# Unread matrix products on TensorE ahead of and inside the expert steps of a conv-attention-MoE kernel

## What is computed

```
probs = softmax(x @ gate_w + gate_b)            # 16 experts
top_probs, top_idx = top_k(probs, 2), made to sum to 1
hidden = silu(x @ w1[e]) * (x @ w2[e])          # 64 -> 128
out    = sum over the two experts e of a token: top_probs * (hidden @ w3[e])
```

## Time and profile before

| what | value |
|---|---|
| median of 3 runs | 426.78 us (426.09 to 432.75) |
| the profiled execution | 428.84 us |
| its span, first to last instruction | 427.0 us |
| mean granted clock of TensorE | 0.835 of full |
| PE / DVE / ACT / POOL busy | 83% / 64% / 43% / 38% of the span |

### The profile page before, as it was taken

The page is one execution under the profiler, slowest core; times in us unless marked ns, Lnnn a source line. Parts: engine busy times, 40 slices in busy tenths (PEclk is TensorE's granted clock), DMA queues, the critical chain, the costliest instruction groups (busy, mean ns, idle before and its releaser), DMA issues. The chain is left out here.

```text
span 427.0 us, 8539 instructions
## 1 busy us (share of the span) xinstructions
PE 355.6 (83%) x2739; PEld 192.9 (45%) x2739; DVE 272.6 (64%) x567; ACT 183.0 (43%) x409; POOL 161.9 (38%) x171
## 2 busy tenths in 40 slices
PE   1588999989999999999999974987851199999970
PEld 0452353343353443534433223676850177777750
DVE  2489977848978879877778996378642033333323
ACT  2684654644646656635656001454311033333330
POOL 3173332332333243233331003015777246666660
PEclk9999999978999999999999997899555555555555
DMA  8859998998885958828859400000002156555415
GB/s 263 337 116 216 322 216 220 343 221 219 202 218 98 218 130 185 232 50 212 204 119 215 114 2 0 0 2 13 27 26 71 38 121 138 123 123 118 107 35 147
DMA packets 55219, 61.50 MB, mean 144 GB/s; under 512 B 23028, under 2 KB 35372, under 8 KB 55056
## 3 DMA queue, kind: packets, MB, share of 16 engines
q1 hardware_dynamic: 43712, 53.52, 49.8%
q10 hardware_dynamic: 8944, 5.41, 4.9%
q0 software_dynamic: 2528, 2.14, 1.6%
HBM read 11.95 MB, written 11.83 MB: 56 GB/s over the span
## 5 line engine op out<-in xcount | busy, mean ns | idle before, releaser
L684 DVE TENSOR_TENSOR prod<-ps_t,a_rep 128x1024 f32<-128x1024 f32 x128 | 151.9, 1218 | 35.9 <-PE ps_t L384 29.8
L791 POOL TENSOR_TENSOR a<-a,mask 128x512 f32<-128x512 f32 (+1 forms) x40 | 46.7, 1169 | 87.8 <-ACT a L544 85.6
L384 PE MATMUL ps_t<-b,vt 32*128 32x512 f32 x512 | 74.0, 647 | 2.1 <-DVE prod L684 2.1
L404 PE MATMUL ps_d<-prod,keep 128*32 128x512 f32 x512 | 69.2, 613 | 3.0 <-DVE prod L684 2.8
L325 PEld LDWEIGHTS ps_m<-om_r,sel 128*128 128x128 f32 x193 | 29.2, 189 | 76.1 <-ACT mask L522 28.2
L1257 POOL DMA_INDIRECT parts<-y_sb,x_in x47 | 45.9, 978 | 35.8 <-issue 25.9
L325 PE MATMUL ps_m<-om_r,sel 128*128 128x256 f32 x193 | 49.6, 336 | 0.0
L768 POOL TENSOR_TENSOR om_r<-om_f,om_r 56x512 fp32r<-56x512 f32 x16 | 20.4, 1273 | 55.4 <-ACT om_r L511 55.3
L1522 PE MATMUL ps_s<-xs,w_in 64*128 64x128 f32 x94 | 37.3, 499 | 0.0
L1523 PE MATMUL ps_p<-xs,w_in 64*128 64x128 f32 x94 | 37.3, 499 | 0.0
L1149 DVE TENSOR_TENSOR hidden<-ps_p,gated 128x128 f32<-128x128 f32 x47 | 13.7, 291 | 36.1 <-ACT gated L1351 36.1
(11 more groups left out here) (151 smaller groups left out, 489.4 us busy)
## 6 DMA issues: line engine op xcount, KB each, us to landing
a_rep<-a SPq DMA_DIRECT2D x128, 256.0 KB, 4.9
rows<-blank SPq DMA_DIRECT2D x8, 1056.0 KB, 6.9
w_in<-in_experts ACTq DMA_DIRECT2D x47, 96.0 KB, 2.1
a_rep<-a SPq DMA_DIRECT2D x32, 128.0 KB, 2.7
x_in<-rows SPq DMA_DIRECT2D x47, 33.0 KB, 1.9
x_in<-rows SPq DMA_DIRECT2D x47, 32.0 KB, 1.8
start<-in_start SPq DMA_DIRECT2D x1, 1344.0 KB, 7.8
parts<-y_sb,x_in POOLq DMA_INDIRECT x47, 2.8
```

The lines of the kernel that those rows point to most:

```text
L384: mm = pe.matmul(out, vt[par][r, v % 2, :, :, :].rearrange("p j y c -> p (j y c)"), b[par][r, pair_taps(v // 2), :].rearrange("p t x -> p ...
L404: mm = pe.matmul(ps_d[r, :], fold[:, v % 2, :], p, start=v == 0, stop=False, skip_group_check=True)
L684: dve.tensor_tensor(p[:, :, :], t[:, :, :], a_rep[par][:, ms, pair_taps(v // 2), :].rearrange("p m t x -> p m (t x)"), ALU.mult).then_inc( ...
L791: pool.tensor_tensor(v, v, mask[(PAIRS * par + k) % 2][:, 0:wide, :], ALU.mult).then_inc(a_done, 1)
```

## The change

Two kinds of product are added whose results nobody reads, and the semaphore of the placing DMAs is split.

1. `keep_busy()`, called after `counts()` and before `turn_in(0)`: PE waits for the last softmax weights (long done) and for the first 26 of the 32 placing DMAs, and then makes `BUSY` = 6 products with the identity as the stationary operand and 512 columns of `prob` as the moving one, into the first bank of `bank_s`.
2. In every `output(s)` one product of two constant tiles, identity (128 x 128) and ones (128 x 128), into 128 columns of `bank_go` that nothing else uses (256 to 383 of the bank of this step). The wait on `y_done` stands ahead of it, the wait on `hidden_done` now behind it.
3. The first 26 placing DMAs add to `placed`, the last 6 to `placed_last`; SyncE waits for both.

```diff
+    BUSY, BUSY_FROM = 6, 26
...
+        ps_go_spare = [bank_go[:, b, 2 * P:3 * P] for b in two]
...
+        placed_last = sem("placed_last")
...
             sp.wait_ge(tab_done, 1)
-            sp.wait_ge(placed, 16 * 2 * TT)
+            sp.wait_ge(placed, 16 * BUSY_FROM)
+            sp.wait_ge(placed_last, 16 * (2 * TT - BUSY_FROM))
...
-                            .then_inc(placed, 16)
+                            .then_inc(placed if 2 * k + w < BUSY_FROM else placed_last, 16)
...
+            def keep_busy():
+
+                pe.wait_ge(exp_done, K * COUPLES)
+                pe.wait_ge(placed, 16 * BUSY_FROM)
+                for _ in range(BUSY):
+                    pe.matmul(bank_s[:, 0, :], ident, prob[:, 0, :, :].rearrange("p t x -> p (t x)"),
+                              start=True, stop=True)
+
...
             def output(s):
                 b = s % WRING
-                pe.wait_ge(hidden_done, s + 1)
                 if positive(s - 1):
                     pe.wait_ge(y_done, s - 1)
+                pe.matmul(ps_go_spare[s % 2], ident, ones, start=True, stop=True)
+                pe.wait_ge(hidden_done, s + 1)
                 pe.matmul(ps_y[s % 2], hidden[s % 2][:, :], w_in[b][:, HIDDEN:HIDDEN + C], start=True, stop=True)\
                   .then_inc(y_ps, 1)
...
             counts()
+            keep_busy()
             turn_in(0)
```

## The result

The changed kernel takes 447.0 us (median of 4 runs, 445.45 to 451.43), the kernel before beside it 427.24 us. The ratio is 1.047 (95% interval 1.042 to 1.052): slower by 19.8 us, which is the predicted 19.8. The interval stands for 18.0 to 22.0 us, so the agreement to a tenth of a microsecond is chance.

The account below looks back on a forecast made before the run. PE at half clock was taken to bound the steps; 46 outputs each 0.43 us later add 19.8 us to the median 426.78, giving 446.6 us. Own range 433 to 460; the 8-in-10 range 420 to 460.

Parts of the forecast that it names:

- What bounds the kernel: In the steps PE sets the pace at 1.56 us each at half clock; POOL allows no less than 1.28 us.
- The split semaphore costs nothing: SyncE's wait before the first x_in: one more instruction, between 0 and a few tenths of a us, taken as 0.
- The six products ahead: Before the steps, in PE's idle time: no cost, clock rising 3 to 6.8 us after their start, ending at 335.6 to 337.4.
- The gap behind them: Between the six products and the steps: a pause of 3.0 to 4.8 us leaves the clock at 0.50.
- The product in every step: On PE between products(s+1) and output(s): 0.43 us more per step at half clock, 46 x 0.43 = 19.8 us.
- the bounds of 0.13 and 0.73: Lowest and highest us per step for the added product at half clock, giving 433 to 460 us in all.
- Does the clock come back inside the steps?: In the steps with the added product: expected no, the clock stays at 0.50.
- The case in which the clock holds: Rival: full clock outlives the pause before the steps, POOL sets 1.28 us a step, 413.5 us; chance 0.11.

Follow-up runs that it names:

- eight_192: Changed kernel with eight products ahead instead of six and a step product of 192 columns of prob instead of 128 of ones: 414.66 us, ratio 0.969.
- ten_both: Changed kernel with ten products ahead instead of six, the step product kept: median 415.94 us, ratio 0.973 to the kernel before.
- ahead_only: Changed kernel without the product in the steps, the six ahead kept: 427.13 us, ratio 0.998 to the kernel before.
- ten_earlier: Changed kernel with ten products ahead, released by the 21st placing DMA instead of the 26th: 446.64 us, ratio 1.044.
- six_later: Changed kernel with the six products released by the 28th placing DMA instead of the 26th: 415.17 us once, 446.62, 447.44 and 447.57 us otherwise.
- ten_192: Changed kernel with ten products ahead and a step product of 192 columns: median 415.07 us, ratio 0.971.
- step_only: Changed kernel without the six products ahead, the product in every step kept: 445.6 us, ratio 1.044 to the kernel before.
- step_256_only: Changed kernel without products ahead and with a step product of 256 columns of prob instead of 128 of ones: 424.02 us, ratio 0.986.

## Why the prediction was right

*What bounds the kernel.* Right. PE set the steps before and after (1.56 and 1.99 us), and POOL's 1.28 us was the floor that ended the gain wherever the clock held (`eight_192`, `ten_both`).

*The split semaphore costs nothing.* `ahead_only` has it and is equal to before, 0.998.

*The six products ahead.* Predicted: no cost, a rise of the clock 3 to 6.8 us after their start, an end 7.3 to 9.1 us after their release. The rise came after 4.3 us and the end after 7.5 us, where the prediction's own prices give 4.3 + (11.2 - 4.3) x 0.52 = 7.9: the price of a 512-column product was a little high. One of the two rises that the range leans on was misread: from 262.3 to 263.08 PE stood idle, so it had worked for 6.0 us and not 6.8 when the clock rose.

*The gap behind them.* Right in its outcome, shown by `ten_both` against `ten_earlier` and by `ahead_only`, and right in size: 336.91 - 333.30 = 3.6 us from the end of the six to the first product, predicted 3.0 to 4.8. The reason given for the outcome was weak, though. I read a limit from single idle times, 1.42 us outlived and 1.47 us not. `six_later` lost the clock behind waits of 1.23, 0.63 and 0.40 us, while `ten_192` kept it through one of 1.04 us. And one stretch of the convolution, the same code behind the same waits of 1.42 and 0.74 us, went both ways. In the kernel before, its last products run at 1.00, and the clock is still at 1.00 for 3 us of the idle time behind them; in the changed kernel the clock falls in the middle of them:

```profile
257.76 1.10 PE L313 MATMUL ps_m<-keep,d_sb 128*128 128x64 f32 x8 [0.74 <-ACT d_sb L550]
...
254.41 1.46 PE L313 MATMUL ps_m<-keep,d_sb 128*128 128x64 f32 x8 [0.74 <-ACT d_sb L550]
...
255.90:260.00 4.10, 0.00 (x0) 0.50 0.00 0
```

The first line is the kernel before, the other two the changed kernel. So no single idle time decides the fall, and behind pauses of about 1 us the clock went either way. With 3.6 us the clock was gone in the profiled execution, and by their times (445.45 to 451.43 us) in the other three as well; with the 2.5 and 0.8 us of `ahead_only` and the 3.58 us of `ten_earlier` too.

*The product in every step.* Predicted 0.43 us at half clock, measured 1.99 - 1.56 = 0.43. Of the bounds of 0.13 and 0.73, neither came near. `step_only` shows that it carries the whole loss. At full clock PE's step was predicted at 1.0 to 1.15 us; `ten_both` shows 1.13.

*Does the clock come back inside the steps?* For 128 columns right: 94 us at 0.50. The reason given was only half a reason. I took 73 us of busy time at 0.50 as a sign that this kind of step can't lift the clock; with 256 columns in it the step did, and by the same reasoning I had expected it not to. That 128 columns fell on the side that stays was a guess that came true.

*The rivals.* The case in which the clock holds was priced at 413.5 us; the three kernels that reach it have medians of 414.7 to 415.9. The statement of the Trainium skill, "TensorE: Matmul & The Clock Gate", Part 1, that activity releases the throttle, agrees with these traces only if activity isn't PE's busy time: that was 93.0 of 94 us at 128 columns, 80.0 of 80 at 192 and 10.0 of 10 at 256 columns while the clock rose.

## What to carry to other kernels

Work that is added to lift TensorE's clock must reach up to the work that is to have it: here a stretch of unread products in front of a wait of some 3 us was lost in the wait. Until the granted clock of a profile shows that it reaches, a filler in the loop is a plain cost on the bounding engine, here 0.43 us a step. Look at every single execution as well as at the median: with 128 or 192 columns in the steps and eight or ten products ahead, one execution in five or six lost the clock. One wide enough to bring it back from half clock should repair such a loss by itself; it did so where the steps began at half clock (`step_256_only`), and no trace shows it behind a loss in the middle of the steps.

## What the runs showed of the hardware

- The same loop can stay at either level of the clock. With 128 columns a step takes 1.99 us at half clock and 1.13 us of PE at full clock (1.28 by POOL), and single executions of one kernel fell on either side: 413.5 and 441.1 us (`ten_both`), 415.2 and 447.6 (`six_later`), and with 192 columns 413.5 and 452.4 (`ten_192`).
- The same waits don't always take the clock: behind 1.42 and 0.74 us in the convolution it fell at 255.0 us in one trace and only 3.4 us into the next idle time in another.
- With fillers of different size and no work ahead, 192 columns stayed at 0.50 for all 47 steps (456.9 us, one execution), 256 came back after about 20 us and 384 after about 6.5 us in their profiled executions, although PE's row in the trace reads busy all the time in each of them.
- The added product takes 0.59 us to the next start where it follows the half-height pair, against 0.43 behind a product like itself, and the output behind it takes 0.32 us instead of 0.48. So whatever stands behind the pair costs 0.16 us more, once a step, with the added product or without it. That the switch between the two forms is the cause wasn't tested by itself.
